# Context rows stored by partition in 24 KB runs, and the last sums of a batch moved behind two value jobs

## The reference

```
# layer 0, attention over the context c, for each batch
scores  = (x W^T + b) (c W^T + b)^T          # 64 x 1601
aligned = softmax(scores) c                  # needs c by rows
# layer 1, attention over the context, for each batch and head h
out_h = softmax(scale * q_h k_h^T) v_h       # k = c Wk^T, v = c Wv^T
```

## Time and profile before

| | |
|---|---|
| median of 3 runs | 1212.67 us (1211.68 to 1213.35) |
| the profiled execution | 1212.91 us |
| its span, first to last instruction | 1211.1 us |
| mean granted TensorE clock | 0.976 of full speed |
| PE busy | 1131.0 us (93%) |
| DVE / ACT / POOL busy | 621.8 / 433.2 / 331.8 us |
| moved by DMA | 115.72 MB |

### The profile page before, as it was taken

The page is one execution under the profiler, slowest core; times in us unless marked ns, Lnnn a source line. Parts: engine busy times, 40 slices in busy tenths (PEclk is TensorE's granted clock), DMA queues, the critical chain, the costliest instruction groups (busy, mean ns, idle before and its releaser), DMA issues.

```text
span 1211.1 us, 34730 instructions
## 1 busy us (share of the span) xinstructions
PE 1131.0 (93%) x15936; PEld 843.3 (70%) x15936; DVE 621.8 (51%) x979; ACT 433.2 (36%) x824; POOL 331.8 (27%) x362
## 2 busy tenths in 40 slices
PE   6979879879799999999999999999999999999897
PEld 3434334358478888888888888888878878865673
DVE  2011158653612545555555654554565564476667
ACT  1010043223232533533443433533443543434342
POOL 0000000012200144333424424333333334264512
PEclk9989989989799999999999999999999999999999
DMA  9998982162200200200200110111110110320000
GB/s 353 365 413 319 390 313 109 39 240 100 85 18 23 71 20 25 71 19 25 71 19 24 54 38 24 37 37 35 43 37 19 59 37 20 127 81 2 20 1 35
DMA packets 38883, 115.72 MB, mean 96 GB/s; under 512 B 2505, under 2 KB 3017, under 8 KB 34641
## 3 DMA queue, kind: packets, MB, share of 16 engines
q1 hardware_dynamic: 38736, 113.50, 26.1%
HBM read 112.44 MB, written 1.05 MB: 94 GB/s over the span
## 4 chain that ended last, share of the span: by engine, by line
PE 77%; DVE 6%; SPq 5%; DMA 4%; POOL 3%; issue 3%; ACT 2%; POOLq 0%; DVEq 0%; ACTq 0%
PE SB L431 46%; PE SC L1181 5%; PE SB L422 5%; SPq L591 4%; PE SB L1211 3%; DMA R<-in_ctx_t 2%; PE SB L1247 2%; PE SB L1000 2%; DMA R<-in_ctx 2%; PE SC L1190 1%; PE SB L1068 1%; POOL CW L748 1%; PE SC L976 1%; PE SB L1056 1%; PE SB L1230 1%
## 5 line engine op out<-in xcount | busy, mean ns | idle before, releaser
L1695 ACT COPY R<-SB 64x512 f32<-64x512 f32 (+1 forms) x224 | 116.5, 520 | 199.1 <-PE SB L431 197.4
L1498 DVE TENSOR_REDUCE LN<-SC 128x64 f32<-128x768 f32 x128 | 116.6, 952 | 130.6 <-PE SC L1181 130.6
L431 PE MATMUL SB<-high,whigh 128*128 128x512 f32 (+2 forms) x512 | 180.1, 352 | 1.0 <-ACT Z L444 1.0
L431 PE MATMUL SB<-high,wlow 128*128 128x512 f32 (+2 forms) x512 | 178.6, 349 | 0.0
L431 PE MATMUL SB<-low,whigh 128*128 128x512 f32 (+2 forms) x512 | 177.5, 347 | 0.0
L431 PE MATMUL SB<-wlow,high 128*128 128x512 f32 (+1 forms) x416 | 165.8, 399 | 0.0
L431 PE MATMUL SB<-whigh,high 128*128 128x512 f32 (+1 forms) x416 | 164.6, 396 | 0.0
L431 PE MATMUL SB<-whigh,low 128*128 128x512 f32 (+1 forms) x416 | 164.2, 395 | 0.0
L734 POOL TENSOR_TENSOR added<-LN 128x768 f32<-128x768 f32 x32 | 58.8, 1838 | 258.6 <-ACT LN L1727 258.6
L734 POOL TENSOR_TENSOR added<-Z 128x768 f32<-128x768 f32 x32 | 58.7, 1834 | 250.5 <-ACT Z L1727 250.5
L431 PEld LDWEIGHTS SB<-high,whigh 128*128 128x128 f32 x512 | 96.7, 189 | 13.2 <-issue 1.4
(11 more groups left out here) (230 smaller groups left out, 1832.3 us busy)
## 6 DMA issues: line engine op xcount, KB each, us to landing
R<-in_ctx_t SPq DMA_DIRECT2D x32, 1024.0 KB, 8.4
R<-in_ctx SPq DMA_DIRECT2D x8, 3072.0 KB
R<-in_ctx_t SPq DMA_DIRECT2D x16, 644.0 KB, 6.5
R<-in_f SPq DMA_DIRECT2D x4, 2048.0 KB, 15.6
R<-in_f SPq DMA_DIRECT2D x1, 8192.0 KB, 24.9
R<-in_ctx_t SPq DMA_DIRECT2D x12, 512.0 KB, 3.6
R<-in_Wk SPq DMA_DIRECT2D x3, 1024.0 KB, 9.8
R<-in_Wv SPq DMA_DIRECT2D x3, 1024.0 KB, 9.0
```

What stands on the lines that cost most here:

```text
L431: last = pe.matmul(out_, lhs[a][:, k, :], rhs[b][:, k, :], start=n == 0, stop=n == 3 * NC - 1)
L1498: inc(dve.tensor_reduce(tops[:, r * T:(r + 1) * T], sc_head[:, :, r, 0:6 * T].rearrange("p g (a q) -> p q g a", q=T), AX.XY, ALU.max), "ha ...
L1695: last = act.copy(keys[nu][64 * half:64 * half + 64, pairs, first * P:first * P + full], src[:, :, 0:full])
```

## The change

Two edits, independent of each other.

1. The host stores the first 1536 context rows of a batch so that the 12 rows of a partition stand behind one another (24 KB), and the 65 last rows in an array of their own. L590 then copies 24 KB to each of 128 partitions; L591 still copies 2 KB to each of 65. What lies in on-chip memory is the same as before.
2. In `BATCH4[1]` to `BATCH4[6]` the step `z -1` stands just before `e 0`, thus behind `w 11` and `w 12`. `BATCH4[0]` and `LAST4` are as they were.

```diff
@@ attention
         order.append(("b", pr))
-        if pr == 0 and outputs:
-            order.append(("z", -1))
         split()
         fill(5.5 if outputs else 4.6, ("e", pr))
+        if pr == 0 and outputs:
+            order.insert(order.index(("e", 0)), ("z", -1))
@@ load_rows
-                    inc(sp.dma_start(dst[:, 0:MF, :], ctx_[b, 0:MF * P, :].rearrange("(t p) d -> p t d", p=P)), name, 16)
-                    inc(sp.dma_start(dst[0:MR, MF, :], ctx_[b, MF * P:M, :]), name, 16)
+                    inc(sp.dma_start(dst[:, 0:MF, :], ctx_[b]), name, 16)
+                    inc(sp.dma_start(dst[0:MR, MF, :], ctx_end[b]), name, 16)
@@ laid_out
-        "x": inputs["x"], "ctx": ctx, "W0": inputs["L0_xattn_W"],
+        "x": inputs["x"], "ctx": ctx[:, :MF * P].reshape(B, MF, P, D).transpose(0, 2, 1, 3),
+        "ctx_end": ctx[:, MF * P:], "W0": inputs["L0_xattn_W"],
```

More of the change, by code:

```diff
@@ L291, with build @@
 MID = 4
-def build(nc, x, ctx_, W0, vecs, Wk, Wv, Wr, Wo, ctrl, f1, f2, Wq4, Wk4, Wv4,
+def build(nc, x, ctx_, ctx_end, W0, vecs, Wk, Wv, Wr, Wo, ctrl, f1, f2, Wq4, Wk4, Wv4,
           Wp4, bp4, Wq5, Wk5, Wv5, Wo5, wq, ws, bq, W0t, ctxt, tie, out):
```

## The result

The changed kernel takes 1199.56 us in the median of six runs (1194.68 to 1202.33), the kernel before 1212.18 us in six runs (1208.93 to 1213.35). The ratio is 0.9908, 95% interval 0.9886 to 0.9930: faster by 11.2 us, from 8.5 to 13.8.

A forecast was written before the change was run, and what follows sets the result against it. Loads were taken to bound the kernel to about 155 us, PE and the vector engines after that. From the profiled 1212.91 us, 5.5 for the rows and 4.8 for z -1 gave 1202.6 us, range 1199.3 to 1208.6.

The forecast's parts named there:

- The packet term: Row loads: each packet costs about 9 ns beside 0.037 ns a byte, so 24 KB runs reach 428 GB/s for 387.
- s: Time saved on loading one batch's 1536 rows with 24 KB runs: 0.78 us, from 8.13 to 7.35.
- step (a): First stage: four batches of rows stand ahead of piece 3 of pair 0, all gained, 4 s = 3.1 us.
- step (c): Rows of pair 2 add 2 s before s3, whose end moves by 6 s = 4.7 us to 134.0.
- step (e): Start of o3: released by o2's side and no longer by a load, at 149.45 us, 5.5 us saved.
- The dips: Rate drops at each batch's end, at the 65-row piece, about 0.5 us each, expected to stay as they are.
- Rival (2): At the batch ends of the row loads the rate drops vanish too: s becomes 1.3, time 1199.5 us; chance 0.10.
- the margins on DVE: Behind the moved z -1, DVE is done with reciprocal and product 1.0 us before the tops of s1.
- The bound I gave: Upper limit of the saving from moving z -1: 5.0 us, six waits of 0.8 and rounding.
- (1): Row loads: rate doesn't hang on run length, or runs stay cut; rows give nothing, 1208.1 us; chance 0.15.
- (3): Row loads: the rate falls with coarse 24 KB packets, 1230 us at 288 GB/s; chance 0.07.
- (4): Layer 1 attention: the wait removed by moving z -1 returns at m 1, behind DVE's reciprocal; 1207.4 us; chance 0.10.

The follow-up runs named there:

- edit 1 alone: The changed kernel with z -1 back straight behind b 0, so only the rows by partition against the kernel before: 1203.13 us, ratio 0.9948.
- once more: The changed kernel itself, nothing altered, timed again beside the kernel before: 1200.81 us, ratio 0.9920 (0.9896 to 0.9944).

## Why the prediction was right

**The packet term** was right: s rests on a line through rates that other loads had, and rows with 4, 8, 24 and 26 KB runs then had 409, 423, about 424 and 426 GB/s where the prediction's rows and line have 412, 420, 428 and 428. The times with 4 and 8 KB came out at its 3.7 and 4.6 us to 0.2 us, though their intervals reach 1.8 us to either side. The estimate by the 3 cycles a packet of the Trainium skill, "DMA: Bandwidth & Descriptors", section "Why small descriptors are slow (HBM only)" (4.4%, by its own cycles 804 / 771 rather 4.3%; 2.7 us for edit 1), does not agree with the trace, which has about 9.5% from 2 to 24 KB, and the 2.7 us lie outside the interval of edit 1 alone, 4.2 to 8.3.

**What reaches the end.** Over four profiles with 2 KB runs and four with 24 KB, piece 3 of pair 0 lands at 66.3 and at 63.5 us in the mean: step (a) had 3.1 us, 2.8 came (3.2 in the pair of profiles above). Piece 3 of pair 3 moves by 5.6 us in that pair and by 5.2 in the mean, where step (c) had 4.7, and o3, whose step (e) had 5.5, by 6.35 in the pair and by 5.8 in the mean of the four (154.7 and 148.9). So the four batches ahead of step (a) gave 0.7 us each, and the two of pair 2 gave more than 1. What is missing behind step (a) may be a term that I had not seen: after o0 the queue is empty when the rows of pair 2 are issued, and starts slower with 2 KB runs. In the six microseconds from L590's issue the kernel before moves 3 x 166 + 3 x 324 GB/s, 1.47 MB; the kernel after moves 1.94, half a megabyte more, of which up to 0.39 MB (a packet for each of 16 engines) can be the booking of whole packets. The kernel with 2 KB runs by partition moves 1.55, with 407 in the second half. So the size of this term, and whether the run or the addresses make it, stay open. Step (e): o3 does wait for o2's side and no longer for the load, as written; 149.45 was forecast, 148.57 came, and 148.9 in the mean.

**The dips.** "I leave them" at 0.5 us each was wrong: they stay, and go from about 0.4 to about 0.7 us each with 24 KB runs. By the windows some 0.3 us of each batch's 0.78 is lost in this way; by where piece 3 of pair 0 lands it is only 0.1, and four profiles a side, which lie up to 2.9 us apart, don't settle it. Some 0.8 us more than the forecast's 2 s came back between that piece and piece 3 of pair 3, where the queue starts empty. That two errors of opposite sign leave o3 at 5.8 us for 5.5 is in part luck. Rival (2) has the right time for the wrong reason.

**Edit 2.** The wait went and nothing took its place, and the margins on DVE (1.0 us) were met to a few hundredths. The size was short: 5.1 to 5.6 us by the third part of the spans, for 4.8. I took PE's own waits, whose ends are modelled; the step from L1190 to the scores of s 1 went from 7.29 to 6.41 us in batch 1 and from 7.35 to 6.42 in batch 2, some 0.9 each. The bound I gave, 5.0, was too tight.

**The rivals.** (1) falls by the 424 GB/s, with which the trace also goes against the 358 GB/s a core of the Trainium skill, "DMA: Bandwidth & Descriptors", section "Where 436 GB/s comes from". (3) falls: the rate rose. (4) falls by z -1 behind s 1. Of the 3.0 us between 1202.6 and 1199.56 these terms are 0.6 to 1.65 (0.3 to 0.85 for the rows, 0.3 to 0.8 for z -1). The rest is not told apart from the scatter of the executions: the forecast counts from one profile, 1212.91 us, with 0.87 of the clock in its second part. By ratio 11.2 us (8.5 to 13.8) and, once more, 9.7 (6.8 to 12.6) were saved, for 10.3 forecast.

## What to carry to other kernels

Where a queue of loads binds, read its rate window by window, each with one kind of run: two or three such rows give the price of a packet, and with it what a longer run is worth; here all that is seen was had with 8 KB. With large packets keep the window away from the ends of a transfer. Then follow each wait through the queue and count how many of the quicker transfers stand ahead of it; only the last wait's count is won, less what PE needs itself. A small job that waits for a slow helper can go behind work that is ready, if what hangs on its result is late, and if the engine that finishes it has the room; look for that room in the idle time just ahead of its next urgent instruction.

## What the hardware showed

- One VectorE operation of 2.28 us (float32 tensor_tensor, both operands and the result in on-chip memory and none of them in PSUM, 128 x 2048) held a GpSimd addition beside it: 2.55 us for 0.46, and when the split was moved, 3.14 for 1.85. Beside a VectorE copy and a reciprocal that read PSUM the second addition took its usual 1.84. The wait that came of it was booked on GpSimd.
- Packets of 2, 4, 8, 24 and 26 KB to 128 partitions moved at 387, 409, 423, 413 to 433 and 426 GB/s in the steady stretch of a batch; at 2 KB the order of the addresses made no difference to this rate. (Behind the empty queue 2 KB packets also went at 408 to 412 GB/s for three microseconds, from 102 us in the kernel before, and then at 391.) A 2 KB piece to 65 partitions between such transfers costs some 0.4 us with 2 KB packets about it and some 0.7 us with 24 KB packets, by the bytes missing in the window.
- The windows book a 24 KB packet whole at one moment: the same rows read 439 GB/s from 21 to 29 us and 428 from 23 to 28.
- Identical instruction streams took 159.3 to 166.1 us in the middle stage, with mean granted clocks of 0.94 to 0.87. That scatter, 6.8 us, is over half of the effect that was sought; the part of the span that holds the clock at full speed (867.0 to 868.0 us over the kernels with edit 2) tells more than the total.
